# First attention of an audio tower: value products alternate between column halves, and the softmax is divided out at the end

## The reference

```
qkv = x @ in_w.T + in_b
q, k, v = jnp.split(qkv, 3, axis=-1)
q, k, v = (sp(q), sp(k), sp(v))          # (batch, head, position, 8)
att = jax.nn.softmax(jnp.einsum('bhqd,bhkd->bhqk', q, k) / jnp.sqrt(jnp.float32(dh)), axis=-1)
o = jnp.einsum('bhqk,bhkd->bhqd', att, v).transpose(0, 2, 1, 3).reshape(B, S, D)
return o @ out_w.T + out_b
```

## Time and profile before

| | us |
|---|---|
| median of 3 runs (2029.08 to 2030.49) | 2029.88 |
| the profiled execution | 2025.78 |
| its span, first to last instruction | 2023.7 |
| PE busy in the span | 1919.9 (95%) |
| DVE, ACT, POOL busy | 1635.6, 1475.7, 1340.8 |

### The profile page before, as it was taken

The page is one execution under the profiler, slowest core; times in us unless marked ns, Lnnn a source line. Parts: engine busy times, 40 slices in busy tenths (PEclk is TensorE's granted clock), DMA queues, the critical chain, the costliest instruction groups (busy, mean ns, idle before and its releaser), DMA issues.

```text
span 2023.7 us, 43887 instructions
## 1 busy us (share of the span) xinstructions
PE 1919.9 (95%) x11396; PEld 1508.8 (75%) x11396; DVE 1635.6 (81%) x4899; ACT 1475.7 (73%) x3083; POOL 1340.8 (66%) x1560
## 2 busy tenths in 40 slices
PE   5996649999999999999999999999999999999997
PEld 3984437777777777777777777777777777777776
DVE  3563658888888888888888888888888888888886
ACT  3663247777778777778777787777777777777875
POOL 2440127777777777777777777777777777777775
PEclk9998759999999999999999999999999999999999
DMA  3000030000100020001000100002000100020001
GB/s 99 1 0 0 1 105 21 20 20 19 60 18 14 19 63 20 20 20 60 18 17 17 62 20 20 20 20 62 20 17 17 57 20 20 20 62 20 18 18 28
DMA packets 118151, 58.03 MB, mean 29 GB/s; under 512 B 109713, under 2 KB 116049, under 8 KB 116814
## 3 DMA queue, kind: packets, MB, share of 16 engines
q1 hardware_dynamic: 115298, 56.75, 10.4%
q10 hardware_dynamic: 2795, 0.70, 0.2%
HBM read 24.55 MB, written 0.70 MB: 12 GB/s over the span
## 4 chain that ended last, share of the span: by engine, by line
PE 82%; issue 3%; POOL 1%; DVE 1%; ACT 0%; DMA 0%; SPq 0%; DVEq 0%; POOLq 0%; ACTq 0%
PE ps L990 28%; PE ps L998 15%; PE ps L981 15%; PE ps L1002 8%; PE ps L1040 4%; PE ps L1058 3%; PE ps L975 2%; PE ps L1050 2%; PE ps L1025 2%; PE ps L1012 1%; PE ps L1018 1%; POOL k_W_low L1335 1%; PE ps L1041 0%; DMA k_X<-k_spl 0%; DVE k_W L1449 0%
## 5 line engine op out<-in xcount | busy, mean ns | idle before, releaser
L1449 DVE SCALAR_TENSOR_TENSOR k_W<-ps,k_W 128x688 f32<-128x688 f32 x1028 | 892.4, 868 | 236.0 <-ACT k_W L1161 209.2
L1335 POOL TENSOR_TENSOR k_W_low<-k_W,k_W_high 128x688 fp32r<-128x688 f32 x513 | 851.5, 1660 | 334.1 <-ACT k_W_high L1166 334.1
L1161 ACT ACTIVATE k_W<-ps 128x688 f32<-128x688 f32 x1029 | 765.6, 744 | 376.1 <-PE ps L981 358.8
L990 PE MATMUL ps<-k_W,k_tab 128*128 128x344 f32 x2048 | 676.7, 453 | 0.0
L981 PE MATMUL ps<-k_X,k_sel 128*128 128x344 f16 x2058 | 472.6, 311 | 24.3 <-DMA k_X<-k_spl 13.3
L990 PEld LDWEIGHTS ps<-k_W,k_tab 128*128 128x128 f32 x2048 | 366.5, 190 | 127.4 <-issue 0.5
L1166 ACT ACTIVATE k_W_high<-k_W 128x688 fp32r<-128x688 f32 x513 | 395.5, 771 | 0.0
L998 PE MATMUL ps<-k_W_high,k_tab_high 128*128 128x344 f32 x1024 | 385.9, 379 | 0.0
L998 PE MATMUL ps<-k_W_high,k_tab_low 128*128 128x344 f32 x1024 | 324.9, 320 | 0.0
L981 PEld LDWEIGHTS ps<-k_X,k_sel 128*128 128x128 f16 x2058 | 176.1, 99 | 195.5 <-issue 91.8
L1002 PE MATMUL ps<-k_W_low,k_tab_high 128*128 128x344 f32 x1024 | 244.2, 319 | 0.0
(11 more groups left out here) (223 smaller groups left out, 2488.0 us busy)
## 6 DMA issues: line engine op xcount, KB each, us to landing
k_tab<-in_tables SPq DMA_DIRECT2D x9, 2048.0 KB, 7.2
k_X<-k_spl SPq DMA_TRANSPOSE x390, 2.4
k_xs<-x2T SPq DMA_DIRECT2D x33, 172.0 KB, 2.1
k_qT<-k_qs SPq DMA_DIRECT2D x33, 86.0 KB, 2.0
cst<-in_consts SPq DMA_DIRECT2D x1, 1024.0 KB, 18.9
wts<-in_weights SPq DMA_DIRECT2D x1, 896.0 KB, 13.0
cst<-in_consts SPq DMA_DIRECT2D x1, 874.5 KB, 16.5
xr<-in_xrows SPq DMA_DIRECT2D x1, 750.0 KB
```

What stands on the lines that cost most here:

```text
L990: mm = mm_(sums, tab[:, slot, at + k, :], W[:, d % RING, k, :], start=(d == 0 and k == 0), stop=(d == NDC - 1 and k == 1))
L1161: A(W[:, d % RING, :, :], ps[:, 2 * (d % 2):2 * (d % 2) + 2, 0:LOUT], ACT.Exp).then_inc(e_done, 1)
L1335: G.tensor_tensor(W_low[:, q % SPLIT_RING, :, :], W[:, d % RING, :, :], W_high[:, q % SPLIT_RING, :, :].bitcast(F32), ALU.subtract).then_i ...
L1449: V.scalar_tensor_tensor(W[:, d % RING, :, :], ps[:, 2 * (d % 2):2 * (d % 2) + 2, 0:LOUT], 0.0, W[:, d % RING, :, :], ALU.is_ge, ALU.mult) ...
```

## The change

- A tile is now one head `j` of each half in both batches, instead of four heads of one batch. Scores still contract 128 rows. The eight value products of a step go to partitions 0 and 64 in turn (`b2` is the innermost loop), in banks 6 and 7 by `hf`.
- `vz` has 64 + 8 columns per head; beside the values stand columns of ones, at the other 32 partitions of the output, so that the same products give the sums of the exponentials. GpSimd writes the ones once.
- The exponentials are no longer summed, divided, or scaled: the factor `DH ** -0.5` goes into the mask (`heads`), and the row maximum is the exponential's bias directly.
- The pipeline is a step shorter: transposes of tile `t` in step `t`, values of `t - 1`.
- The output leaves PSUM by a VectorE copy (`take_outputs`); ScalarE makes the reciprocal of the sums by a logarithm and an exponential (`invert_sums`); GpSimd multiplies (`divide_by_sums`). Twice a pass.
- The bias of V goes through the projection into `bo`, by a product with one column at the start.
- The first feed-forward product goes to the two row halves in turn.

The diff, cut to its core (left out: buffers and semaphores, the writing of the ones, the new layout in `feed_values`, and the relus' bank numbers):

```diff
+                def divide_by_sums(p, qt):
+                    q0, m = QT[qt]
+                    o = oT[:, bass.ds(p, 1), q0:q0 + m].rearrange("p a s -> p (a s)")
+                    pool.wait_ge(rz_ready, 4 * p + (2 * qt + 2))
+                    pool.wait_ge(vz_ready, 4 * p + 8)
+                    for g in range(4):
+                        hf, at = g % 2, 32 * g
+                        a = nc.gpsimd.tensor_tensor(o[at:at + 32], oz[at:at + 32, qt, hf, 0:m], rz[at:at + 32, qt, 0:m], ALU.mult)
+                    a.then_inc(oT_ready, 1)
...
-                        for t in range(8):
-                            n = QT[t // 4][1]
-                            pool.wait_ge(rz_ready, 8 * p + t + 1)
-                            nc.gpsimd.tensor_tensor(P[0:n, t % 4, :, :], P[0:n, t % 4, :, :],
-                                                    rz[0:n, t % 4, :, None].to_broadcast([n, 4, S]), ALU.mult).then_inc(pn_ready, 1)
-                            if t == 2:
-                                pool.wait_ge(score_done, 8 * p + 1)
-                                feed_keys(1 - par, following)
-                            if t == 4:
-                                pool.wait_ge(pv_done, 8 * p + 1)
-                                feed_values(1 - par, following)
+                        pool.wait_ge(score_done, 8 * p + 1)
+                        pool.wait_ge(oT_ready, 2 * p + 2)
+                        feed_keys(1 - par, following)
+                        pool.wait_ge(pv_done, 8 * p + 1)
+                        feed_values(1 - par, following)
+                        for qt in range(2):
+                            divide_by_sums(p, qt)
...
+                nc.tensor.matmul(ps[:, 3, 400:401], weight("o1"), bias("bv1"), start=True, stop=True).then_inc(bo_mm, 1)
...
                 def scores(par, t):
-                    qt, b2, hf = t // 4, (t // 2) % 2, t % 2
+                    qt, j = t // 4, t % 4
                     q0, n = QT[qt]
-                    for j in range(4):
-                        mm = nc.tensor.matmul(ps[0:n, 2 * hf + j // 2, (j % 2) * S:(j % 2 + 1) * S],
-                                              qz[:, par, b2, 4 * hf + j, q0:q0 + n], kp[:, par, :], start=True, stop=True)
+                    for hf in range(2):
+                        for b2 in range(2):
+                            mm = nc.tensor.matmul(ps[0:n, 2 * (t % 2) + b2, hf * S:(hf + 1) * S],
+                                                  qz[:, par, b2, 4 * hf + j, q0:q0 + n], kp[:, par, :], start=True, stop=True)
                     mm.then_inc(score_done, 1)
 
                 def turn_probabilities(k, t):
-                    hf, n = t % 2, QT[t // 4][1]
-                    pe.wait_ge(pn_ready, k + 1)
+                    n = QT[t // 4][1]
                     pe.wait_ge(pt0_ready, k + 1)
                     pe.wait_ge(pt1_ready, k + 1)
...
                     mm.then_inc(ptr_done, 1)
 
                 def values(k, par, t):
 
-                    qt, b2, hf = t // 4, (t // 2) % 2, t % 2
+                    qt, j = t // 4, t % 4
                     n = QT[qt][1]
                     pe.wait_ge(pt0_ready, k + 2)
                     pe.wait_ge(pt1_ready, k + 2)
-                    for j in range(4):
-                        for kt, (k0, kn) in enumerate(QT):
-                            at = 128 * (4 * hf + j) + 64 * b2
-                            mm = nc.tensor.matmul(ps[64 * b2:64 * b2 + 64, 6 + qt, 0:n], vz[0:kn, par, kt, at:at + 64],
-                                                  PT[0:kn, hf, kt, 95 * j:95 * j + n],
-                                                  start=(hf == 0 and j == 0 and kt == 0), stop=(hf == 1 and j == 3 and kt == 1))
+                    for kt, (k0, kn) in enumerate(QT):
+                        for hf in range(2):
+                            for b2 in range(2):
+                                g = 2 * b2 + hf
+                                mm = nc.tensor.matmul(ps[64 * b2:64 * b2 + 64, 6 + hf, 0:n], vz[0:kn, par, kt, b2, hf, 64 * j:64 * j + 64],
+                                                      PT[0:kn, t % 2, kt, 95 * g:95 * g + n],
+                                                      start=(j == 0 and kt == 0), stop=(j == 3 and kt == 1))
                     mm.then_inc(pv_done, 1)
...
-                            if t >= 1:
-                                turn_probabilities(8 * p + (t - 1), t - 1)
+                            turn_probabilities(8 * p + t, t)
                             if t == 1:
                                 pe.wait_ge(vz_ready, 4 * p + 4)
-                            if t >= 2:
-                                if t in (2, 6):
-                                    pe.wait_ge(oT_ready, 2 * p + (t // 4 + 1))
-                                values(8 * p + (t - 2), par, t - 2)
-                        turn_probabilities(8 * p + 7, 7)
-                        values(8 * p + 6, par, 6)
+                            if t >= 1:
+                                if t in (1, 5):
+                                    pe.wait_ge(oz_ready, 2 * p + (t // 4 + 1))
+                                values(8 * p + (t - 1), par, t - 1)
                         values(8 * p + 7, par, 7)
...
-                for b2 in range(2):
-                    for hf in range(2):
-                        for g in range(2):
+                for hf in range(2):
+                    for g in range(2):
+                        for b2 in range(2):
...
                 def exponentials(t):
-                    hf, n = t % 2, QT[t // 4][1]
-                    for j in range(4):
-                        a = nc.scalar.activation(P[0:n, t % 4, j, :], ps[0:n, 2 * hf + j // 2, (j % 2) * S:(j % 2 + 1) * S],
-                                                 ACT.Exp, bias=ebias[0:n, hf, j:j + 1], scale=DH ** -0.5,
-                                                 accum_out=Z[0:n, t % 4, j:j + 1])
+                    n = QT[t // 4][1]
+                    for b2 in range(2):
+                        for hf in range(2):
+                            g = 2 * b2 + hf
+                            a = nc.scalar.activation(P[0:n, t % 2, g, :], ps[0:n, 2 * (t % 2) + b2, hf * S:(hf + 1) * S],
+                                                     ACT.Exp, bias=negmax[0:n, t % 2, g:g + 1])
                     a.then_inc(exp_done, 1)
 
...
-                    def copy_output(qt):
-                        q0, m = QT[qt]
-                        act.wait_ge(pv_done, 8 * p + (4 * qt + 4) + 1)
-                        nc.scalar.activation(oT[:, bass.ds(p, 1), q0:q0 + m].rearrange("p a s -> p (a s)"),
-                                             ps[:, 6 + qt, 0:m], ACT.Identity, bias=bias("bv1")).then_inc(oT_ready, 1)
+                    def invert_sums(qt):
+                        m = QT[qt][1]
+                        act.wait_ge(oz_ready, 2 * p + (qt + 2))
+                        for g in range(4):
+                            hf, at, sums = g % 2, 32 * g, 32 * (g + 1 - 2 * (g % 2))
+                            a = nc.scalar.activation(rz[at:at + 32, qt, 0:m], oz[sums:sums + 32, qt, hf, 0:m], ACT.Ln)
+                        a.then_inc(rz_ready, 1)
+                        act.wait_ge(rz_ready, 4 * p + (2 * qt + 1))
+                        nc.scalar.activation(rz[:, qt, 0:m], rz[:, qt, 0:m], ACT.Exp, scale=-1.0).then_inc(rz_ready, 1)
 
                     for t in range(8):
-                        if t >= 1:
-                            copy_turned(t - 1)
-                        act.wait_ge(ebias_done, 8 * p + t + 3)
+                        copy_turned(t)
+                        if t == 6:
+                            invert_sums(0)
+                        act.wait_ge(max_done, 8 * p + t + 3)
                         exponentials((t + 2) % 8)
-                        if t == 6:
-                            copy_output(0)
-                    copy_turned(7)
-                    copy_output(1)
+                    invert_sums(1)
...
+                dve.wait_ge(bo_mm, 1)
+                V.tensor_scalar(bo[:, :], ps[:, 3, 400:401], bias("bo1"), None, ALU.add).then_inc(bo_ready, 1)
...
-                    dve.wait_ge(max_done, k + 1)
-                    V.tensor_scalar(ebias[0:n, hf, :], negmax[0:n, hf, :], DH ** -0.5, None, ALU.mult).then_inc(ebias_done, 1)
...
...
+                def take_outputs(p, qt):
+                    m = QT[qt][1]
+                    dve.wait_ge(pv_done, 8 * p + (4 * qt + 4) + 1)
+                    dve.wait_ge(oT_ready, 2 * p + (qt + 1))
+                    V.tensor_copy(oz[:, qt, :, 0:m], ps[:, 6:8, 0:m]).then_inc(oz_ready, 1)
+
+                V.tensor_scalar(heads[:, :], const("batch_head"), DH ** -0.5, None, ALU.mult).then_inc(heads_step, 1)
+                dve.wait_ge(heads_step, 1)
...
-                            n = QT[t // 4][1]
-                            dve.wait_ge(exp_done, 8 * p + t + 1)
```

(31 more changed lines are left out.)

43 lines of the change are left out of this document (23 added, 20 removed).

## The result

| us | before | after |
|---|---|---|
| median of the runs | 2029.60 (4 runs) | 2009.01 (4 runs) |
| lowest and highest | 2029.08 to 2030.49 | 2007.59 to 2010.72 |
| the profiled execution, its span | 2025.78, 2023.7 | 2008.43, 2006.6 |

The ratio of after to before is 0.9898, with an interval from 0.9881 to 0.9916: faster by 1.0%, some 20.6 us. The forecast was 2009.7.

The account below looks back on a forecast made before the run. TensorE was taken to set the pace of the first attention's loop. Start +2.0, loop -23.4, end +2.4, feed-forward -2.2, clock +1.0 sum to -20.2 us, from a median of 2029.88 to 2009.7; range 2003 to 2018.

Parts of the forecast that it names:

- The halves overlap: First attention's loop: a step's value products go from 1.46 to 0.82 us, the step from 3.57 to 2.93.
- Rival A: Value products: nothing overlaps, steps stay at 3.57 us, 2029.7 us in all, no change; chance 0.04.
- Rival C: Value products: changing halves costs each record its whole latency, a step of 6.0 us, 2109 in all; chance 0.03.
- The end of a pass: End of each loop pass: the last values wait 0.2 us (0 to 0.9) for copies; a pass takes 23.65.
- rival B: Loop: ScalarE or VectorE becomes the bound through longer small operations; passes of 26 us give 2019; chance 0.05.
- The start: Before the loop: VectorE waits for the bias product, so masks and scores begin later; +2.0 us (0.8 to 3.5).
- The end: Between loop and projection: copy, logarithms, exponential, multiplies and hand-overs take 3.0 us; +2.4 (1.5 to 3.5), once.
- The clock behind the gap: Idle time before the projection may put the layer norm at the lower clock; +1.0 us (-1 to +4).
- The feed-forward: First feed-forward product alternates row halves, ScalarE's relus then set its end; -2.2 us (-2.6 to -1.2).
- The total: Whole kernel: -20.2 us, giving 2005.6 for the profiled execution and 2009.7 for the median; chance 0.88.

Follow-up runs that it names:

- the kernel with one half: Changed kernel with both batches' value products sent to the same column half, second batch's output not computed: 2028.54 us, ratio 1.0006.
- by fours: Changed kernel with the value products alternating between the column halves in groups of four records: 2010.55 us, one run.
- ten idle instructions: Changed kernel without division, with 14 against 4 short exponentials without a reader behind ScalarE's attention loop: 2007.52 us with 14, 2024.79 with 4.
- by eights: Changed kernel with a step's value products ordered as eight records for one column half, then eight for the other: 2020.32 us, one run.
- the first five products added: Changed kernel plus five products without a reader ahead of the projection: 2010.19 us, one run.
- all eight and the bias later: Changed kernel plus products without a reader, five ahead of the projection and three behind the normalisation, and bias read between the masks: 2004.42 us, ratio 0.9887.

## Why the prediction was right

- **The halves overlap.** Forecast 0.82 for a step's values, 2.93 for a step; measured 0.81 and 2.92. Rival A is refuted by the kernel with one half, which is what A describes: 2028.54. The rule of the Trainium skill ("TensorE: Matmul & The Clock Gate", section "Part 3: Packing small matmuls") that a weight load overlaps only into other row groups would have given 1.46 in both kernels; both halves use the same rows, and only the column half differs between the two. I was wrong to hold the Trainium skill against the change, though. That rule fits neither kernel: loads and products on the same rows overlap before the change too (106.30 and 114.21 us busy of 118.05). And the table of the same section gives three products in different column groups (32 output columns each, 512 moving) 2.38 times the speed, which speaks for the change and which I passed over. Rival C would have shown steps of 6.0.
- **The end of a pass.** Forecast 0.2 of waiting per pass; the trace has 0.9 for the weight load's wait on VectorE's copy, in four times, the longest 0.2, and the average pass took 93.35 / 4 = 23.34. With 23.65 I was 0.3 too high, and the loop gave 24.8 instead of 23.4: a pass takes no longer than eight steps of 2.92, which are 23.36. Exponentials without a sum start every 0.30 us, the lower bound; copies, logarithms and exponential took 1.4, as estimated. Nothing of rival B is seen.
- **The start.** Forecast +2.0, measured +1.97, but otherwise made up: the masks began at 35.16 and the scores at 38.68, and of the lower clock for the first scores I had put 0.4 of 1.4, while they took 1.7 longer. The exponentials and maxima of the first tiles gained 1.4 where I had put 0.4, so two errors of the forecast cancel here, and that its sum is right is luck.
- **The end.** Forecast +2.4, measured +3.3. The mis-sized term is the GpSimd multiply of 32 x 95: 0.39 us each, where I took 0.25; four make 0.6. The hand-overs between the engines are the other 0.2. The copy took 0.35, as estimated.
- **The clock behind the gap.** Forecast +1.0; from projection to feed-forward +1.8. It was the term with the widest bounds (-1 to +4), and it is mis-sized by 0.8.
- **The feed-forward.** Forecast -2.2, measured -2.5, of which the order is 1.4 to 1.7. The rest is not the change's own: before, 3.4 us of this stage lay at the lower clock, and in the changed kernel none. The relus stand back to back, as forecast (150.74, eight in 3.89).
- **Not foreseen:** 1.6 us in the main loop's turns, where ScalarE's sequencer is silent for 3.1 to 3.5 us behind the branch instead of 2.6 to 2.7, and 1.5 us at the kernel's end.
- **The total.** Up to the second feed-forward product the forecast was -20.2 and -20.26 was measured, but only because errors cancel: the loop gave 1.4 more and the feed-forward 0.3 more than forecast, and the end of the attention and the clock behind it cost 1.7 more. For the profiled execution the forecast was 2005.6 and 2008.43 was measured, 2.8 more. For the median it was 2009.7 and 2009.01: I had added the 4.1 us by which the median of the kernel before lay above its profiled execution, and in the changed kernel that distance is 0.6. So the mechanism and the size of its main term were right, and that the median came out within 0.7 us is luck.

What stays open: what ScalarE fetches in the second silence, and why the first is 3.1 to 3.5 us in the changed kernel and 2.6 to 2.7 in the one before. No kernel without any such pause was built.

## What to carry to other kernels

Products with 64 output columns should go to the two column halves in turn, in groups of four records or fewer: 16 records of 95 columns then take 0.81 us (by fours 0.86) instead of 1.46, although both halves use the same rows. A long wait of an engine that nobody waits for is worth nothing (66.0 us removed, 0.0 gained), while one of 3.8 us on TensorE costs itself and, with the clock that fell behind it, 1.8 more. And where a program has loops, read the turns of each build before comparing two of them: ten idle instructions on one engine were worth 17 us.

## What the runs showed of the hardware

- TensorE runs records for the two column halves side by side, and by eights one half's first record started while the other's last three, which stand ahead of it, had not yet started (told apart by their rows, 95 and 94). By eights the gain was 0.27 us of 1.46, by fours 0.60, in turn 0.65.
- ScalarE's pause at a loop's turn was 3.3 to 3.6 us in the changed kernel and 7.0 to 7.8 with ten instructions fewer ahead of the loop. It has two parts: one right behind the branch, in every kernel (2.6 to 3.5), and one at a fixed place of the program (2.9 to 5.2), which appears when that place lies four or eight instructions behind the loop's start.
- Where the stretches at 1.2 GHz fall differs between profiles: 138.2 to 145.0 us in the changed kernel, 149.6 to 153.0 with the first five products added, and with all eight and the bias later none between 31.7 and 161.4.
